# Attention loop: high parts ahead of the query block on ScalarE, output's low part behind the row maximum on VectorE, statistics behind the norm's low part

## What is computed

```python
def _L0_attn_a_ref(x, wq, wk, wv, wo):      # 16 heads, 4 key heads, head size 128
    ...
    scores = jnp.einsum('bhtd,bhsd->bhts', q, k_full) / np.sqrt(HEAD_DIM)
    mask = _sink_window_mask(t)[None, None, :, :]   # (k <= q) & ((k < 4) | (k >= q - 31))
    attn = _masked_softmax(scores.astype(jnp.float32), mask).astype(x.dtype)
    out = jnp.einsum('bhts,bhsd->bhtd', attn, v_full)
    out = out.transpose(0, 2, 1, 3).reshape(b, t, N_HEADS * HEAD_DIM)
    return out @ wo.T
x = x + _L0_attn_a_ref(_layernorm(x, axis=-1), ...)
x = x + _L0_ffn_ref(_layernorm(x, axis=-1), ...)
x = x + _L0_attn_b_ref(_layernorm(x, axis=-1), ...)
x = x + _L0_ffn_ref(_layernorm(x, axis=-1), ...)
```

## Time and profile before

| | us |
|---|---|
| median of 3 runs | 539.81 |
| lowest, highest | 539.01, 540.2 |
| profiled execution | 538.82 |
| its span | 537.0 |
| busy over the span: PE, PEld | 510.3, 427.7 |
| busy over the span: DVE, ACT, POOL | 407.6, 313.3, 149.5 |

### The profile page before, as it was taken

How to read it: one execution, slowest core, us unless ns; L and a number is a source line. 1 busy time by engine, 2 the same in 40 slices (tenths; PEclk the granted TensorE clock), 3 DMA queues, 4 the chain that set the end, 5 groups by cost and what they waited for, 6 DMA issues and landing times. The chain is left out here.

```text
span 537.0 us, 9053 instructions
## 1 busy us (share of the span) xinstructions
PE 510.3 (95%) x2957; PEld 427.7 (80%) x2959; DVE 407.6 (76%) x901; ACT 313.3 (58%) x783; POOL 149.5 (28%) x300
## 2 busy tenths in 40 slices
PE   5999999999999989999999999999898999999996
PEld 4778899999998978678887888757787768888784
DVE  5626565665566898899988999966887779898777
ACT  3656878588587754674443545989762354443342
POOL 2232425244242320110010204568533120010110
PEclk9999999999999999999999999999999999999999
DMA  7320100000001204000030000000000000000101
GB/s 276 116 81 1 40 2 2 1 1 2 2 2 64 90 1 142 1 1 0 1 139 0 1 1 1 1 1 1 1 1 2 0 1 1 1 0 1 40 1 39
DMA packets 5789, 14.23 MB, mean 27 GB/s; under 512 B 624, under 2 KB 2928, under 8 KB 5744
## 3 DMA queue, kind: packets, MB, share of 16 engines
q1 hardware_dynamic: 5744, 13.67, 7.3%
HBM read 12.62 MB, written 1.05 MB: 25 GB/s over the span
## 5 line engine op out<-in xcount | busy, mean ns | idle before, releaser
L172 PE MATMUL psum<-xT_hl,ffn_w_hl 128*128 128x512 f32 x312 | 77.8, 396 | 1.4 <-ACT f_sil L1170 0.6
L172 PE MATMUL psum<-f_um,ffn_w_hl 128*128 128x512 f32 x288 | 72.7, 399 | 1.1 <-DVE f_t L1284 0.5
L172 PEld LDWEIGHTS psum<-xT_hl,ffn_w_hl 128*128 128x128 f32 x312 | 56.1, 188 | 14.1 <-issue 2.0
L172 PEld LDWEIGHTS psum<-f_um,ffn_w_hl 128*128 128x128 f32 x288 | 53.2, 188 | 14.7 <-DVE f_um L1296 1.4
L1170 ACT ACTIVATE f_sil<-psum 128x512 f32<-128x512 f32 (+1 forms) x48 | 28.2, 595 | 48.8 <-PE psum L172 48.8
L1194 ACT ACTIVATE f_ch_hl<-f_ch 128x512 fp32r<-128x512 f32 x48 | 30.3, 631 | 45.0 <-DVE f_ch L1353 44.8
L701 DVE TENSOR_TENSOR pT_hl<-psum,pT_hl 126x360 fp32r<-126x360 f32 (+1 forms) x44 | 23.6, 536 | 41.3 <-ACT pT_hl L608 41.3
L172 PE MATMUL psum<-wo_hl,oT_hl 128*128 128x256 f32 x384 | 50.7, 281 | 4.2 <-DVE oT_hl L707 2.6
L172 PEld LDWEIGHTS psum<-wo_hl,oT_hl 128*128 128x128 f32 x384 | 47.8, 188 | 7.1 <-DVE oT_hl L707 5.2
L172 PE MATMUL psum<-xT_hl,wq_hl 128*128 128x512 f32 x192 | 52.1, 407 | 0.6 <-ACT qT L574 0.6
L574 ACT ACTIVATE qT<-psum 128x512 f32<-128x512 f32 x32 | 34.9, 1091 | 29.0 <-PE psum L172 29.0
(11 more groups left out here) (257 smaller groups left out, 1149.6 us busy)
## 6 DMA issues: line engine op xcount, KB each, us to landing
w_raw<-in_wq SPq DMA_DIRECT2D x4, 512.0 KB, 3.5
w_raw<-in_wo SPq DMA_DIRECT2D x4, 512.0 KB, 3.3
ffn_w_raw<-in_ffn SPq DMA_DIRECT2D x3, 576.0 KB, 5.0
ffn_w_raw_far<-in_ffn SPq DMA_DIRECT2D x3, 576.0 KB, 5.4
ssd_w_raw<-in_ssd SPq DMA_DIRECT2D x3, 512.0 KB, 4.6
x_resid<-in_x SPq DMA_DIRECT2D x2, 512.0 KB, 4.7
out_x<-x_resid SPq DMA_DIRECT2D x4, 256.0 KB, 2.1
w_raw<-in_wk SPq DMA_DIRECT2D x1, 512.0 KB, 6.9
```

What stands on the lines that cost most here:

```text
L172: i = e.matmul(dst, lhs(a), rhs(b), start=start and n == 0, stop=stop and n == len(TERMS) - 1, **kw)
```

## The change

Three edits, none of which adds or removes an instruction. In ScalarE's loop the copy of a query block moves behind the two high parts of the same step. In VectorE's loop the output's low part moves from behind pT's low part to directly behind the row maximum, and from step 43 (`NU - 1`) on to the front of the step. And at the seam the statistics of the tile added in step 45 are taken in step 46, behind the norm's low part, instead of in step 45 behind the addition.

```diff
 # act
                 for i in range(STEPS):
-                    for n in q_chunk.get(i, ()):
-                        q_evac(n)
                     if 0 <= i - LAG_P < NU:
                         pT_hi(i - LAG_P)
                     if 0 <= i - LAG_F < NU:
                         oT_hi(i - LAG_F)
+                    for n in q_chunk.get(i, ()):
+                        q_evac(n)
                     if NF <= i < NU:
                         exps(i)
 # dve
+                def added_stats(i):
+                    if i in y_tile and y_tile[i] >= (KV - 1) * NT:
+                        early(phase, "stats", e, y_tile[i] % NT)
+
                 for i in range(STEPS):
+                    if i >= NU - 1 and 0 <= i - LAG_F < NU:
+                        oT_lo(i - LAG_F)
                     if NF <= i < NU:
                         row_max(i)
+                    if i < NU - 1 and 0 <= i - LAG_F < NU:
+                        oT_lo(i - LAG_F)
                     if NF <= i < NU + 1:
                         recip(i - 1)
                     if 0 <= i - LAG_P < NU:
                         pT_lo(i - LAG_P)
-                    if 0 <= i - LAG_F < NU:
-                        oT_lo(i - LAG_F)
                     if i == NU + 1:
                         early(phase, "norm0", e)
                     if i in y_tile:
                         add(y_tile[i])
-                        if y_tile[i] >= (KV - 1) * NT:
-                            early(phase, "stats", e, y_tile[i] % NT)
-                    for step, stage in ((NU, "veps0"), (NU + 2, "lo0"), (NU + 3, "logits_copy0"), (NU + 4, "split0")):
+                    if i == NU + 2:
+                        early(phase, "lo0", e)
+                        added_stats(i - 1)
+                    if i != NU + 1:
+                        added_stats(i)
+                    for step, stage in ((NU, "veps0"), (NU + 3, "logits_copy0"), (NU + 4, "split0")):
                         if i == step:
                             early(phase, stage, e)
```

## The result

| | us |
|---|---|
| median after (7 runs, 535.78 to 537.96) | 537.13 |
| median before, beside it (7 runs) | 539.87 |
| ratio, 95% interval | 0.9951 (0.9939 to 0.9963) |
| profiled execution after, its span | 537.13, 535.3 |

The change makes the kernel 2.7 us faster (2.0 to 3.3 by the interval); 2.26 had been forecast. In the code of the changed kernel the attention's lines are those of before; the lines behind line 740 stand nine further down.

The account below looks back on a forecast made before the run. The prediction took TensorE to bound the attention, with gains only where it waits for ScalarE or VectorE. Gains of 1.83 and 0.43 us, together 2.26, took 539.81 to 537.55 us, range 536.3 to 539.0.

Parts of the forecast that it names:

- Term 1: Middle of the attention: ScalarE's earlier high parts remove three TensorE waits for the addition, 3 x 0.61 = 1.83 us gained.
- Term 2: End of the attention: VectorE's earlier low parts and later statistics bring the last projection forward, 0.43 us gained.
- The walk: Attention's end, timed on the clock of before: 1.50 us lead at step 44, 0.50 loss at the transposes, 0.43 lead finally.
- One sign to look for: End of the attention: TensorE would wait 1 us or more ahead of the transposes near 196 us.
- the end eats its gain: Rival, 15%: at the end, VectorE's wait behind unit 43's exponentials costs 0.50 us and nothing comes back; 538.5 us.
- Late additions: Rival, 7%: VectorE's reciprocals or pT part keep the three mid-attention additions late; no measurable change, 539.4 us.
- late queries: Rival, 7%: the two copies delay the query copy at six places where queries follow queries, 4.5 us lost; 542.05 us.
- The lead of step 44: Rival, 6%: unit 43's exponentials don't hold unit 39 back, so the end keeps 1.5 us; 536.5 us.

Follow-up runs that it names:

- the third of the orders: Changed kernel, but in step 44 VectorE does the addition, then unit 39's low part, then statistics and variance, ahead of the rest; median 537.5 us, ratio 0.9964.
- the fourth of the orders: Changed kernel with unit 38's low part behind step 43's maximum, and step 44 ordered addition, unit 39's low part, statistics, variance; median 537.31 us, ratio 0.9961.

## Why the prediction was right, step by step

**Term 1** was 3 x 0.61 = 1.83 and measured 0.64 + 0.62 + 0.65 = 1.91: the steps at which the scores of after gain on those of before are 16, 27 and 38, the three places named, and ScalarE's edit alone has them. The working behind it holds in the rows above: no wait, 0.56 from scores to projection where 0.55 was said, and 0.6 us of room for the addition. The copy of the queries was costed at nothing and cost nothing: the copies ahead of it were to end near 88.5 on the clock of before, and they end at 89.25, which is 88.50 on that clock (0.75 taken off). What the working said wrongly is that the copies run in ScalarE's idle time; they run in the time that the exponentials have left. For the exponentials ahead of it as well the room is not enough: that cost 3.1 us.

**What term 1 left out**: 0.27 us at steps 6 and 7. In the trace of before, p·v of unit 1 waited for pT's low part; VectorE's row, and TensorE's:

```profile
59.51 0.53 DVE L701 TENSOR_TENSOR pT_hl<-psum,pT_hl 126x360 fp32r<-126x360 f32 x1 [2.55 <-ACT pT_hl L608]
```

```profile
59.27 0.81 PE L475 MATMUL psum<-k_windows,qT 128*120 128x66 f32 x6 [0.22 <-issue]
60.09 0.76 PE L172 MATMUL psum<-pT_hl,v_hl 126*128 126x360 f32 x3
```

TensorE's starts are 0.82 apart, 0.63 in the kernel after, and the idle column shows nothing, because the row of the scores reaches to 60.08. The rest lies in the projection of step 6, which takes 1.48 to the next start and 1.38 after; before, its first weight load had stood 0.28 for the output's low part (63.03), and after it has no such wait. The prediction looked at waits that a view names, and only between starts that it had already picked; a comparison of all starts behind scores would have shown this one. ScalarE's edit alone has it too (0.38).

**Term 2** was 0.43 and measured 2.62 - 2.17 = 0.45 (the scores of step 39 stand 2.17 ahead, the last projection 2.62, both behind the first scores). The walk, with 1.17 taken off (the 2.17, less the 1.00 by which after's first scores stand later), and what the rows show:

| | walked | measured |
|---|---|---|
| projection of step 44 | 190.06 | 190.03 |
| the addition behind it | 193.75 | 193.68 |
| next projection | 194.32 | 194.24 |
| transposes | 196.90 | 196.82 |
| projection behind | 198.52 | 198.47 |
| last projection | 203.78 | 203.76 |

VectorE's wait for ScalarE's copy was said to be 1.1 and was 1.18. One sign to look for was put in the wrong place: TensorE's wait of over 1 us stands ahead of the projection of 194.24 (1.72), not ahead of the transposes (0.16). The walk had it so, the closing list did not. The working charged the third edit with 0.2 and had its good side within the 0.63 of the projection behind the transposes; undone, it takes 0.43 away, all of the end's net gain, so it was the edit that mattered there. The term was right for edits 2 and 3 together; edit 2, under which the walk stands, gave nothing by itself.

**The sum**: 2.26 forecast, 2.62 in D and 2.7 in the medians. The difference in D is the 0.27 of steps 6 and 7 and 0.08 of term 1. That the medians gave as much as D is in part luck: measured again, they were 2.1 apart. By the idle column the three waits would have been worth 1.26, and they were worth 1.91. The Trainium skill, Perfetto Trace Analysis, section Identifying the Most-Contended Engine, says that matmul busy time is not a good measure, because pipelined instructions look smaller in the trace. The trace agrees only with the first half, and the prediction took it for both: here the rows look larger than what they are worth, since the idle column shows 0.42 where 0.64 was lost.

**The rivals.** That the end eats its gain fell by 0.45; where the third edit is missing, the end gains nothing (0.03 of D), but the loss of 0.50 that the rival had came in no run. Late additions and late queries fell by the rows. The lead of step 44 was not kept, but what that rival claimed was to be had: by another order of the same instructions the last projection comes 1.09 earlier than in the changed kernel. What the rival had wrong is its condition: the exponentials of unit 43 did hold unit 39 back, and the order that took the gain works around that.

## What to carry to other kernels

When two engines evacuate one bank in turn, order them together: VectorE's two edits gained 0.4 us behind ScalarE's and lost 3.3 without it, because an engine that waits in order holds all that it could have done meanwhile. Before an instruction is moved forward, look at every engine that takes its results in order, the third one too: here a reciprocal pair put behind the variance held up a root on GpSimd that doesn't read it. Measure starts, not idle columns, and take a distance inside the changed part when the whole time moves by other causes of the same size.

## What the runs showed of the hardware

**The granted clock, near 415 us.** The medians of some kernels were over a us higher than their D said. A part of that goes with executions in which the mean granted clock is 0.997. ScalarE's edit alone, by stretch:

```profile
410.00:415.00 5.00, 3.97 (x35) 3.73 (x34) 3.54 (x10) 2.12 (x4) 0.60 (x2) 0.99 0.02 3
415.00:420.00 5.00, 5.00 (x20) 4.11 (x19) 2.98 (x9) 0.45 (x1) 1.20 (x3) 0.66 0.00 0
```

and its rows on TensorE:

```profile
413.01 1.05 PE L1792 MATMUL psum<-const_f,gated_sq 128*128 128x1 f32 x8 [1.03 <-DVE x_resid L2027]
...
414.72 0.28 PE L172 MATMUL psum<-ssd_w_out_hi,g_hi 128*128 128x256 f32 x1
414.84 0.32 PE L172 MATMUL psum<-ssd_w_out_lo,g_hi 128*128 128x256 f32 x1
414.95 0.41 PE L172 MATMUL psum<-ssd_w_out_hi,g_lo 128*128 128x256 f32 x1
415.17 0.41 PE L172 MATMUL psum<-ssd_w_out_hi,g_hi 128*128 128x256 f32 x1
```

Ahead of this stand eight transposes (from 410.95), the idle time of 1.03 and eight matmuls of one column (413.01). The matmuls then start at 0.12 from one to the next, and from 414.95 on at 0.21: from 2.4 to 1.2 GHz. In the changed kernel's first profile the same idle time stands at 411.8, and the clock stayed at 1.00. By medians, executions at 0.997 took 1.1 us more than those at 1.00 in ScalarE's edit alone (538.84 and 537.75), and 0.8 more in the changed kernel (537.9 and 537.06), 1.3 when it was measured again (538.0 and 536.67); the 1.5 of the expectation was too much. Executions at 0.997 were 6 of 10 in ScalarE's edit alone, 9 of 10 with the third edit undone, 6 of 7 in the third of the orders, and of the changed kernel 2 of 7 and later 4 of 6; of the kernel before, 1, 4, 6 and 2 of 19, 19, 11 and 9. With the four matmuls in the gap (the idle time there is 0.17) it was none of 16, in three kernels (four of them showed 0.999). That the clock keeps up near 415 us with the gap filled is shown as far as 16 executions go, against 4 of 6 of the changed kernel and 6 of 11 of the kernel before beside them; why the kernels differ in how often they lose it, though the gap is the same in all, stays open. Nor is the clock the whole of it: executions at 1.00 of one kernel lie up to 1.9 us apart (535.7 to 537.58 in the fourth of the orders), of which the start ahead of the first scores can have one (38.5 to 39.7 us in the profiles); the rest is open too.

**VectorE beside GpSimd.** In the changed kernel the guard of the reciprocals (120x3), 0.16 us elsewhere, took 1.30:

```profile
89.73 1.30 DVE L661 TENSOR_SCALAR small<-small 120x3 f32<-120x3 f32 x1
```

while GpSimd made a weight's low part:

```profile
88.61 2.40 POOL L383 TENSOR_TENSOR wq_hl<-w_raw,wq_hl 128x1024 fp32r<-128x1024 f32 x1 [1.82 <-ACT wq_hl L379]
```

It ended when GpSimd did (91.03 and 91.01), and the same stood at 128.48 beside GpSimd's 127.36 to 129.75; with 1.03, 1.31 and 1.32 at 63.46, 111.21 and 149.98 that makes five, one for each of the five low parts of weights that GpSimd makes in that time. Before, the longest was 0.37; in ScalarE's edit alone it was 1.97. No wait of TensorE stands at these places, since VectorE had room. The Trainium skill, SBUF — State Buffer, section Who interferes with whom, says that VectorE and GpSimd share a pair of ports as an exclusive lock, that tensor_scalar can take it, and that the one that comes second waits for the whole instruction of the other. The rows agree.
